# Inverse transform along the height: 32 products of 104x104 a group become 128 products on 64x64 quarters of the array

## What is computed

```python
def _spectral_conv(x, w):                       # x: (B, 32, 64, 64)
    x_ft = jnp.fft.rfft2(x, norm='ortho')
    out = jnp.einsum('bixy,ioxy->boxy', x_ft[:, :, :M1, :M2], w.astype(x_ft.dtype))   # M1 = M2 = 20
    out_ft = jnp.zeros((B, w.shape[1], H, W // 2 + 1), dtype=x_ft.dtype)
    out_ft = out_ft.at[:, :, :M1, :M2].set(out)
    return jnp.fft.irfft2(out_ft, s=(H, W), norm='ortho')
x = coords @ fc0_w + fc0_b
x = jnp.transpose(x, (0, 3, 1, 2))
for sw, cw, cb in ((sw0, cw0, cb0), (sw1, cw1, cb1), (sw2, cw2, cb2), (sw3, cw3, cb3)):
    x1 = _spectral_conv(x, sw)
    x2 = jnp.einsum('bchw,oc->bohw', x, cw) + cb[None, :, None, None]
    x = _gelu(x1 + x2)
```

## Time and profile before

| | |
|---|---|
| median of the runs | 6577.88 us (6573.84 to 6582.02) |
| the profiled execution's own time | 6565.23 us |
| its span, first to last instruction | 6563.4 us |
| TensorE matmul, busy | 5753.6 us, 88% of the span |
| TensorE weight loads, busy (beside matmul) | 4399.3 us, 67% |
| VectorE, ScalarE, GpSimd, busy | 44%, 41%, 17% |
| granted TensorE clock, mean | 0.94 (0.97 to 0.98 up to 5000 us, 0.83 behind) |

### The profile page before, as it was taken

How to read it: one execution, slowest core, us unless ns; L and a number is a source line. 1 busy time by engine, 2 the same in 40 slices (tenths; PEclk the granted TensorE clock), 3 DMA queues, 4 the chain that set the end, 5 groups by cost and what they waited for, 6 DMA issues and landing times. The chain is left out here.

```text
span 6563.4 us, 235714 instructions
## 1 busy us (share of the span) xinstructions
PE 5753.6 (88%) x100766; PEld 4399.3 (67%) x100766; DVE 2862.4 (44%) x4334; ACT 2661.3 (41%) x4948; POOL 1096.6 (17%) x1048
## 2 busy tenths in 40 slices
PE   5999999998998999999999998998995777877777
PEld 4887788688868876887788688868873434243333
DVE  2443444344434443443444344434442737465563
ACT  2334433433353334334433533353333737354553
POOL 3220322022222212220322032222210000000000
PEclk9999999999999999999999999999997888888887
DMA  2101101111101111101111110101101000000000
GB/s 32 13 13 14 18 13 13 15 17 16 20 9 23 13 13 19 13 13 13 18 13 13 15 17 13 23 7 21 15 3 21 1 7 1 0 7 1 4 1 4
DMA packets 442544, 82.73 MB, mean 13 GB/s; under 512 B 437305, under 2 KB 437577, under 8 KB 441417
## 3 DMA queue, kind: packets, MB, share of 16 engines
q1 hardware_dynamic: 441544, 67.56, 8.2%
HBM read 63.31 MB, written 4.23 MB: 10 GB/s over the span
## 5 line engine op out<-in xcount | busy, mean ns | idle before, releaser
L217 POOL COPY x_T<-x_X 128x512 f32<-128x512 f32 x1024 | 1067.4, 1101 | 3736.3 <-ACTq L718 3565.8
L713 ACT ACTIVATE x_X<-ga 128x512 f32<-128x512 f32 x1280 | 751.2, 597 | 899.7 <-PE ga L433 693.9
L591 DVE COPY x_X<-ev 128x512 f32<-128x512 f32 x640 | 442.6, 692 | 1281.7 <-PE ev L451 1217.7
L433 PEld LDWEIGHTS ga<-pw_rhs,x_X 64*64 64x64 f32 x32768 | 608.1, 135 | 303.1 <-issue 300.0
L681 ACT ACTIVATE V<-ga 104x512 f32<-104x512 f32 x416 | 248.4, 597 | 1043.7 <-PE ga L401 1043.7
L401 PE MATMUL ev<-inv_h,D 104*104 104x128 f32 x4864 | 617.8, 276 | 36.9 <-DVE D L591 35.9
L433 PE MATMUL ga<-pw_rhs,x_X 64*64 64x64 f32 x32768 | 606.0, 218 | 27.3 <-issue 24.2
L591 DVE COPY V<-ev 104x512 f32<-104x512 f32 x608 | 420.5, 692 | 471.0 <-PE ev L401 471.0
L401 PEld LDWEIGHTS ev<-inv_h,D 104*104 104x104 f32 x4864 | 560.0, 171 | 72.8 <-DVE D L591 27.0
L463 PEld LDWEIGHTS ev<-dft_consts,x_T 128*64 128x64 f32 x16384 | 575.0, 137 | 42.9 <-issue 42.9
L463 PE MATMUL ev<-dft_consts,x_T 128*64 128x80 f32 x16384 | 594.9, 233 | 6.2 <-POOL x_T L217 5.6
(11 more groups left out here) (192 smaller groups left out, 7674.3 us busy)
## 6 DMA issues: line engine op xcount, KB each, us to landing
mix_w<-in_sw SPq DMA_DIRECT2D x128, 400.0 KB, 8.2
coords<-in_coords SPq DMA_DIRECT2D x64, 96.0 KB, 2.1
maps<-Y SPq DMA_DIRECT2D x128, 16.0 KB
raw<-maps SPq DMA_DIRECT2D x8, 256.0 KB, 3.5
out<-out_t SPq DMA_DIRECT2D x8, 256.0 KB, 3.1
w<-in_w SPq DMA_DIRECT2D x3, 512.0 KB, 6.6
fc_rhs<-in_fc_w SPq DMA_DIRECT2D x32, 0.4 KB
dft_consts<-in_dft SPq DMA_DIRECT2D x1, 336.0 KB
```

The lines of the kernel that those rows point to most:

```text
L217: pool.tensor_copy(x_T[:, :, H * bc + h0:H * bc + h0 + 16].rearrange("p c (s n) -> p c s n", n=2), blocks.rearrange("p (s a n c) -> p a c ...
L433: last = pe.matmul(ps[HALF * bp:HALF * bp + HALF, HALF * s:HALF * s + HALF], x_X[r:r + HALF, g, col:col + HALF], pw_rhs[r:r + HALF, :], st ...
L591: dve.tensor_copy(dst, src).then_inc(ev_taken, 1)
L713: x_new = act.activation(blocks.rearrange("p (s a n) -> p s a n", s=8, a=2)[:, :, bc, :], ga[n % N_GA][:, :].rearrange("p (s n) -> p s n", ...
```

## The change

The old function stays as `inverse_h_rows`, on all three engines, and is used as before for the first group of every pass and in the last layer. In the second to fourth group of the mid passes a new `inverse_h` takes its place. For each channel it issues four products: the image pair in the low or high rows of `D` (`bp`, 40 rows each) times the first or second image of the last axis (`bc`, 64 or 40 columns), with a 40x64 piece of `inv_h` as moving data. Each lands on its own 64x64 quarter of the array. The low rows write an `ev` bank, the high rows a `ga` bank, and 8 channels fill such a pair, so there are 4 pairs instead of 8 single banks. Each pair has two waits, each followed by `passed()`. Copies out are as many as before (4 by VectorE, 4 by ScalarE, 512 elements on 104 partitions), with 64x8 elements each where there were 128x4.

```diff
@@ tensor
+                def inverse_h(d_at, shared=True):
+
+                    pe.wait_ge(ev_taken, ev0 + d_at[0] + 1)
+                    pe.wait_ge(ga_taken, ga0 + d_at[1] + 1)
+                    for i in range(INV_T // 2):
+                        pair = [ev_tile()]
+                        passed()
+                        pair.append(ga_tile() if shared else ev_tile())
+                        passed()
+                        for s in range(8):
+                            for bp, ps in enumerate(pair):
+                                r = HALF * bp
+                                for bc, m in enumerate((HALF, KR)):
+                                    last = pe.matmul(ps[HALF * bc:HALF * bc + m, HALF * s:HALF * s + HALF],
+                                                     D[r:r + KR, 8 * i + s, HALF * bc:HALF * bc + m],
+                                                     inv_h[r:r + KR, r:r + HALF], start=True, stop=True)
+                                if s == 7:
+                                    last.then_inc(ga_ready if shared and bp else ev_ready, 1)
                     return n["ev"], n["ga"]
...
@@ vector
+                def inverse_h(step=2):
+                    for i in range(0, INV_T, step):
+                        n0, c0 = HALF * (i % 2), 8 * (i // 2)
+                        take(V[0:HALF + KR, n0:n0 + HALF, c0:c0 + 8],
+                             ev_tile()[0:HALF + KR, :].rearrange("p (c n) -> p n c", n=HALF))
...
-                    if more:
-                        inverse_h(1 if kind == "last" else 2)
+                    if more and kind == "last":
+                        inverse_h_rows(1)
+                    elif more:
+                        inverse_h()
...
@@ scalar
+                def inverse_h():
+                    m = n
+                    for i in range(1, INV_T, 2):
+                        act.wait_ge(ga_ready, ga0 + m + 1)
+                        act.activation(V[0:HALF + KR, HALF:P, 4 * i - 4:4 * i + 4],
+                                       ga[m % N_GA][0:HALF + KR, :].rearrange("p (c n) -> p n c", n=HALF), ACT.Copy)\
+                            .then_inc(ga_taken, 1)
+                        m += 1
+                    return m
```

More of the change, by code:

```diff
@@ L392, in turn_d, with inverse_h_rows @@
                     return n["ev"], n["ga"]
-                def inverse_h(d_at, shared=True):
+                def inverse_h_rows(d_at, shared=True):
                     pe.wait_ge(ev_taken, ev0 + d_at[0] + 1)
@@ L403, in inverse_h @@
                         last.then_inc(ga_ready if shared and i % 2 else ev_ready, 1)
+                    return n["ev"], n["ga"]
+                def inverse_h(d_at, shared=True):
[15 more added lines that the diff above has]
+                                    last.then_inc(ga_ready if shared and bp else ev_ready, 1)
                     return n["ev"], n["ga"]
@@ L522, in last_group @@
                         fc1(1)
-                        v_next = inverse_h(d_at, shared=False)
+                        v_next = inverse_h_rows(d_at, shared=False)
                     else:
@@ L539, in run @@
                     passed()
-                    v_at = inverse_h(turn_d(0))
+                    v_at = inverse_h_rows(turn_d(0))
                 if kind == "first":
@@ L616, in turn_d, with inverse_h_rows @@
                             take(D[:, :, k0:k0 + 16], bank.rearrange("p (k c) -> p c k", c=CH))
-                def inverse_h(step=2):
+                def inverse_h_rows(step=2):
                     for i in range(0, INV_T, step):
@@ L649, in run @@
                     turn_d(2)
-                    inverse_h()
+                    inverse_h_rows()
                 else:
@@ L675, in run, with inverse_h_rows @@
                 n = 0
-                def inverse_h():
+                def inverse_h_rows():
                     m = n
@@ L704, in run @@
                         n += 1
-                    n = inverse_h()
+                    n = inverse_h_rows()
                 for g in range(NG):
```

## The result

| | before | with the change |
|---|---|---|
| median of the runs | 6576.84 us (4 runs) | 6726.48 us (6724.38 to 6735.14, 4 runs) |
| ratio, 95% interval | | 1.0229 (1.0211 to 1.0247) |
| span of the profiled execution | 6563.4 us | 6726.6 us |
| mean granted clock | 0.940 | 0.906 |

What follows compares the result with a forecast made beforehand. TensorE was taken to bound the kernel; 3.22 us saved in products less 1.2 us of added instruction waits made 2.0 us a group, x 72 = 145 us, so 6577.9 - 145 = 6433 us, range 6345 to 6540.

Steps and rivals of the forecast that it cites:

- What bounds the kernel: Whole kernel: TensorE is on the path, busy 88% of the time, and the cost of `inverse_h` is paid in full.
- Part 1, the product: `inverse_h` on TensorE: quarter products take 3.95 us instead of 7.17, gaining 3.22 us a group, 232 us over 72 groups.
- Part 2, copies and waits: Copies out to `V` and added waits in `inverse_h`: they keep up, VectorE's at 0.69 us, adding nothing.
- Part 3, the instructions: Instruction supply from `inverse_h` through L433: 512 records in the stage add 1.2 us a group, bounds 0 and 3.2.
- the price of two borders in `mix_next`: Supply pace seen in `mix_next`: 256 records in 3.47 us, 1.06 us of it idle, used for the new stage's supply.
- the slack of `forward_w`: Before `inverse_h`: slow records let supply get ahead, so the stage's first packet border costs between nothing and 0.49 us.
- The clock: Within a group: a fall to 1.2 GHz was named only as a sign of being wrong; no cost was given.
- The rival on the other side: `inverse_h` to L433: supply slows to 4.1 us a packet, 5.2 us added against 3.2 saved, about 6720 us; chance 0.05.

Runs made afterwards that it cites:

- e6: The change with one product over all 104 weight columns in place of two on quarters, and 64 rows (24 zero) instead of 40; 6540.31 us, ratio 0.9928.
- e8: e6 with one of its four pairs of banks, the second, done on full 64x64 quarters; 6508.25 us, ratio 0.9902.
- e9: e6 with two of its four pairs of banks, the second and fourth, done on full 64x64 quarters; 6488.42 us, ratio 0.9878.
- e11: The change with 64 rows (24 zero) in every product and its own 64 or 40 weight columns, run again with rounds; 6657.92 us, ratio 1.0139.
- e10: The change itself run once more, on the same chip as e11; 6742.56 us, ratio 1.0266.
- e4: The change with pairs of banks in turn by full 64x64 quarters (64 rows) and by the old 104x104 products; 6539.5 us, ratio 0.9931.
- e12: e6 with three of its four pairs of banks, the first, third and fourth, done on full 64x64 quarters; 6600.03 us, ratio 1.0042.
- e3: The change with one product over all 104 weight columns (40 rows) in place of two on quarters, half the records; 6693.98 us, ratio 1.0166.
- e2: The change with its quarters filled to 64 rows and 64 weight columns by zeros, same number of instructions; 6652.38 us, one run.
- e7: The change with 64 rows (24 zero) in every product and its own 64 or 40 weight columns; 6658.84 us, one run.
- e1: The change with every quarter product moving 128 columns instead of 64, same number of instructions, V not the reference's; 6659.79 us, one run.
- e5: e4 with 40 rows and 64 or 40 weight columns in its quarter products; 6534.52 us, one run.

## Why the prediction was wrong

The range was 6345 to 6540 us and the forecast 6433; measured 6726. Step by step:

- **What bounds the kernel**: right. TensorE is on the path, and the stage is paid in full; e6, e8 and e9 gain by shortening it.
- **Part 1, the product**: right. A pair takes 0.94 us, 3.76 us the stage; 40 rows run no faster than 64 and no slower, as long as the clock holds.
- **Part 2, copies and waits**: right. VectorE's copies to `V` still take 0.69 us, and TensorE waits for neither of the copying engines in L419.
- **Part 3, the instructions**: the right mechanism at a third of its price, and beyond its own bound. This is the step that failed first. I put the added wait at 1.2 us a group, at most 3.2. e11, where the clock stays up in 65 of 72 groups, has groups of 29.13 us against 28.45 and should have saved 3.2 us in products: 3.9 us were added. The profile marks about 2.2 us of that as idle by "issue"; in the rest the records only start further apart. The sum went by 3.47 us for 256 records, the price of two borders in `mix_next`; the piece between two waits takes 3.80 us here and 3.79 in e11 (206.75 to 210.54 us), and such pieces go up to 4.5 us. Why more than 3.47 is open. I took it that the slack of `forward_w` covers the first border almost wholly; the first wait of the stage is 1.11 us, no shorter than the second (0.86). And I let `forward_h` give something back, where in e11 it takes 3.80 us instead of 2.92 at full clock. In the groups this makes a loss of 0.7 us, 49 us in all, instead of a gain; 41 us more are lost outside them, and together they are the 1.4% of e11 (6658 us).
- **The clock**: missing from the sum, the second step that failed. I named the fall of the clock only as something that would prove me wrong, having seen it fall only behind the idle time at the ends of passes. It now falls in 64 of the 72 groups, for 5.3 us on average over all, which costs some 1.1 to 1.2 us a group (30.19 and 30.37 us in the change and its repeat, against 29.13 in e11) and 84.6 us between e10 and e11.
- **The rest of the kernel**: put at nothing without a word. Outside the 72 groups 38 us were lost, nearly all of it in `mix_next`.
- **The arithmetic of the forecast**: added waits of 0.4 to 2.3 us do give 6376 to 6512 us, but the middle of that is 6444, not 6433. It changes nothing here.
- **The rival on the other side** gave about 6720 us for a supply of 4.1 us for 256 records. The number is near the measured one for half a reason, and that it is so near is luck: without the fall of the clock the time is 6658 us.
- Of the Trainium skill (Runtime: NRT & Kernel Launch, section on instruction fetch mechanics) the block of 256 instructions holds: the waits in e11 come at about that distance, 250 records and the few instructions between them that are not shown. That crossing a border is mostly hidden holds where records come slowly, as in e4 and e9 (52 and 69 a us over the stage), and not at 130 a us, where a border in the group of e11 shown costs 1.1 to 1.4 us.

## What to carry to other kernels

Before a product is cut into smaller ones, count records in a microsecond as well as columns: here TensorE ran freely up to 384 records in 5.6 us and at 448 in 5.4 us lost more than it gained, and half of the stage on quarters beat all of it. Where two forms of a product cost the same, take the one that fills the rows of the array, if need be with zeros that are there anyway: it cost no time here and kept the clock up. A wait that ends by "issue" and comes back after a fixed number of records belongs to the whole stream and not to the line that it stands at: in e12 it came in the stage behind the dense one. Here 0.4 us of it in a group was the sign of a limit that 256 more records in a stage did not run into (e9), and 320 and 384 more did (e12, the change). And look at the parts that an edit doesn't touch: here 27 to 60 us were lost there each time.

## What the runs showed of the hardware

- With the same number of instructions, the granted clock went with how many rows the products fill. 40 of 64 rows, with waits for instructions (the change) or 0.094 us apart without any (e3): on average 5.3 to 5.5 and 4.6 us a group at half clock, in 64 and 56 of the 72 groups. 64 rows with the very same waits (e2, e7, e11) or the same spacing (e6): 1.00, or at most 0.6 us a group at half. 40 rows streaming twice as long a product without much waiting (e1), or in half of the stage only (e5): 1.00. So few rows did not always bring the fall, and the same waits with full rows hardly did; where the border lies was not tried. The Trainium skill (TensorE: Matmul & The Clock Gate, section on what is actually happening) has the clock follow how busy the engine has been; e3, with a matmul running in all of its 7.56 us, shows that busy time as the profile counts it doesn't tell that.
- A product on a quarter costs the same with 40 or 64 rows and with 40 or 64 columns of weights: 0.029 to 0.030 us for one float32 product of 64 columns (0.94 us / 32 in the change and in e11, at full clock). On two row halves with 104 columns of weights a product takes 0.094 us (6.01 us / 64 in e6).
- Two waits for instructions with nothing but quarter products between them are 3.8 to 4.5 us and about 250 records apart (the change, e2, e7, e11).
